# Where the next region's bias tiles stand among the column and row tiles of a sixteen-head mixing kernel

## The reference, cut to what matters

```python
h = relu(nd[..., None] * W1[0] + b1)          # nd: log distance, 0 above the diagonal
x = x + (einsum('qkm,mh->qkh', h, W2) + b2).transpose(2, 0, 1)
ret  = einsum('BGMTS,GMN->BGNTS', x, w + eye)
hq   = einsum('BGMTS,BTGIM->BGITS', x, qw1)   # a matrix for each row t
ret += einsum('BGITS,BTGIM->BGMTS', hq, qw2)
hk   = einsum('BGMTS,BSGIM->BGITS', x, kw1)   # a matrix for each column s
ret += einsum('BGITS,BSGIM->BGMTS', hk, kw2)
ret += x * qdd (by row) + x * kdd (by column)
```

## Time and profile before

| | before |
|---|---|
| median of three runs | 930.36 us (927.4 to 930.49) |
| profiled execution | 932.34 us |
| its span | 930.5 us |
| mean granted TensorE clock | 0.929 |
| TensorE matmul busy | 747.1 us (80%) |
| VectorE / ScalarE / GpSimd busy | 453.0 / 386.3 / 432.1 us |
| DMA moved | 149.63 MB, mean 161 GB/s |

### The profile page before, as it was taken

The page is one execution under the profiler, slowest core; times in us unless marked ns, Lnnn a source line. Parts: engine busy times, 40 slices in busy tenths (PEclk is TensorE's granted clock), DMA queues, the critical chain, the costliest instruction groups (busy, mean ns, idle before and its releaser), DMA issues.

```text
span 930.5 us, 39085 instructions
## 1 busy us (share of the span) xinstructions
PE 747.1 (80%) x18210; PEld 552.8 (59%) x18210; DVE 453.0 (49%) x483; ACT 386.3 (42%) x412; POOL 432.1 (46%) x267
## 2 busy tenths in 40 slices
PE   0667863898779877998899978988789886997974
PEld 0254642676557655766667655666557665766974
DVE  7496522376335543554336623554336542563343
ACT  3959413554445344543343334333434244431200
POOL 3546421254224422455568745675548654681020
PEclk9889977999989999998999999999889998999998
DMA  6786676839972999199844998389744998098068
GB/s 132 181 174 143 153 154 149 180 67 246 252 162 59 220 228 201 48 190 240 197 92 99 225 175 206 58 191 249 169 84 91 214 236 185 19 188 212 6 156 198
DMA packets 301054, 149.63 MB, mean 161 GB/s; under 512 B 30044, under 2 KB 296668, under 8 KB 300892
## 3 DMA queue, kind: packets, MB, share of 16 engines
q1 hardware_dynamic: 187552, 92.05, 45.3%
q10 hardware_dynamic: 113340, 55.08, 26.4%
HBM read 77.61 MB, written 69.47 MB: 158 GB/s over the span
## 4 chain that ended last, share of the span: by engine, by line
PE 70%; issue 12%; SPq 5%; DVE 4%; DMA 3%; ACT 2%; ACTq 2%; POOL 0%; DVEq 0%
PE main L755 27%; PE main L744 25%; PE bias L769 18%; SPq L326 4%; DMA homes<-in_x 2%; ACT homes L513 1%; ACTq L269 1%; DVE homes L299 1%; SPq L334 1%; DVE homes L601 1%; DMA out_mixed<-homes 1%; ACT hidden L502 1%; SPq L269 1%; DVE homes L604 0%; DVE w_blocks L626 0%
## 5 line engine op out<-in xcount | busy, mean ns | idle before, releaser
L463 POOL TENSOR_TENSOR hidden<-log_table,row_scale 128x1024 f32<-128x1024 f32 x192 | 364.4, 1912 | 366.9 <-PE bias L769 359.1
L755 PE MATMUL main<-homes,mats_b 32*32 32x120 f32 (+1 forms) x9216 | 286.6, 273 | 107.6 <-issue 80.1
L755 PEld LDWEIGHTS main<-homes,mats_b 32*32 32x32 f32 x9216 | 260.3, 133 | 173.0 <-issue 137.2
L502 ACT ACTIVATE hidden<-hidden,b_col 128x1024 f32<-128x1024 f32 x192 | 219.2, 1148 | 306.4 <-issue 154.6
L744 PEld LDWEIGHTS main<-homes,mats_a 32*32 32x32 f32 x8192 | 240.8, 129 | 87.1 <-issue 67.1
L744 PE MATMUL main<-homes,mats_a 32*32 32x128 f32 x8192 | 263.5, 276 | 28.6 <-issue 28.4
L669 DVE SCALAR_TENSOR_TENSOR homes<-bias,b_col,homes 64x512 f32<-64x512 f32 (+1 forms) x256 | 185.8, 747 | 119.5 <-PE bias L769 75.1
L769 PE MATMUL bias<-hidden,w_blocks 128*64 128x512 f32 x768 | 208.2, 646 | 19.1 <-ACT hidden L502 9.4
L651 DVE TENSOR_TENSOR homes<-main,homes 128x1024 f32<-128x1024 f32 x128 | 156.7, 1225 | 111.7 <-PE main L744 111.5
L641 DVE COPY homes<-main 128x960 f32<-128x960 f32 x64 | 74.1, 1158 | 231.8 <-PE main L755 231.7
L529 ACT ACTIVATE homes<-main 128x960 f32<-128x960 f32 (+1 forms) x80 | 71.0, 890 | 124.1 <-PE main L755 109.3
(11 more groups left out here) (37 smaller groups left out, 32.2 us busy)
## 6 DMA issues: line engine op xcount, KB each, us to landing
homes<-in_x SPq DMA_DIRECT2D x200, 192.0 KB, 6.7
out_mixed<-homes ACTq DMA_DIRECT2D x192, 192.0 KB
homes<-in_x SPq DMA_DIRECT2D x72, 256.0 KB, 7.2
out_mixed<-homes ACTq DMA_DIRECT2D x72, 128.0 KB, 4.5
homes<-in_x SPq DMA_DIRECT2D x136, 64.0 KB
mats_in<-a_mats SPq DMA_DIRECT2D x128, 64.0 KB
out_mixed<-homes ACTq DMA_DIRECT2D x28, 256.0 KB, 7.5
out_mixed<-homes SPq DMA_DIRECT2D x28, 256.0 KB, 6.7
```

The source lines that it names most:

```text
L463: nc.gpsimd.tensor_tensor(hidden_tile(u, g).rearrange("p (j s) -> p j s", j=ROWS), bass.AP(logs.tensor, logs.offset, [list(logs.ap[0]), [1 ...
L502: nc.scalar.activation(hidden_tile(u, g), hidden_tile(u, g), ACT.Relu, bias=b1_col[:, 0:1])\
L755: mm = pe.matmul(main[of_group(g), i % 2, j * W:j * W + REGION_TILES[k] * ROWS], b_weights(g, C * ROWS + j), y_column(k, g, C * ROWS + j), ...
```

## The change

`bias_step` gets other numbers for k of 1 and more; for k = 0 it stays. Before, the fifteen bias tiles stood after steps 1, 3, 5, ..., 29: eight behind column tiles, seven behind row tiles. Now tiles 0 to 9 stand after steps 1, 2, 4, 5, 7, 8, 10, 11, 13 and 14, two for every three column tiles, and tiles 10 to 14 after steps 17, 19, 21, 23 and 25. Steps 26 to 30 have none.

```diff
@@ -177,7 +177,10 @@
         def bias_step(k, T):
 
-            return 1 + T * (COL_TILES + REGION_TILES[k] - 3) // (REGION_TILES[k + 1] - 1)
+            if k == 0:
+                return 1 + T * (COL_TILES + REGION_TILES[k] - 3) // (REGION_TILES[k + 1] - 1)
+
+            return 1 + 3 * T // 2 if T < 10 else COL_TILES + 2 * (T - 10) + 1
```

## The result

| | before | changed |
|---|---|---|
| median of four runs | 930.24 us (927.40 to 930.49) | 957.52 us (947.98 to 982.57) |
| ratio of the fast runs | | 1.033, 95% interval 1.026 to 1.040 |
| profiled execution, its span | 932.34, 930.5 us | 954.62, 952.8 us |
| mean granted TensorE clock | 0.929 | 0.933 |

The changed kernel is 3% slower. The forecast was 956 us. The ratio leaves out the run of 982.57 us, a slow one; the two medians alone stand at 1.029. Timed once more, beside some of the experiments, the ratio was 1.040 (1.028 to 1.052). The experiments ran on three chips, where the times of a kernel spread by 2% and more, and are told in ratios to the kernel before on the same chip for that reason.

What follows compares the result with a forecast made beforehand. TensorE's order of work and its stops, read as instruction fetches, were taken to bound the kernel. Terms 12.4 + 0 + 10 + 3.5 = 26 us on 932.3 gave 958, median 956 us; range 922 to 978.

Steps and rivals of the forecast that it cites:

- a, the wait for hidden tiles: Column steps, regions 4 to 7: TensorE waits 1.55 us in close bias-tile pairs; eight of twenty counted, 12.4 us.
- the pairs there are covered: Column steps up to 9, regions 4 to 7: three of five close pairs hide within 6.7 us instruction blocks, uncounted.
- The bound of 31 us: Column steps, regions 4 to 7: all twenty waits of 1.55 us are paid if the cover fails.
- b, the two moved bias tiles: Seven regions, two bias tiles each from row to column steps: sum 0, bounds 21 us more or less.
- c, tile 14 and its x: Row steps, regions 1 to 7: bias tile after step 25 meets late x; 16 us summed, 10 taken.
- none in region 5: Row steps of region 5: VectorE does not wait for x before the bias addition after step 25.
- d, tile 1 and its x: Column steps, regions 1 and 5: TensorE stands one column tile earlier when late x lands, 3.5 us in all.
- The reading of the stops as code that arrives late: Column steps: TensorE's stops, 128 matmul records apart, are waits for the next 16 KB instruction packet among x loads.
- faster: Column steps: stops swallow the moved bias tiles and all waits there; 918 to 922 us, chance 0.14.
- Everything is paid: Whole kernel: stops aren't fetches, or come on top; 50 us more, 981 us, chance 0.12.
- The clock, which I feared for: Column steps: granted clock 0.88 against 1.00 in rows; twenty new stops could bring more slow work; no separate size.

## Why the prediction was right

Right was the time (957.5 us against 956; 954.6 against 958 for the profiled execution), the sign and the kind of three of its four terms. How close the number came is in part luck: the terms were off by several microseconds each, in both directions, and the ratio was 1.040, or 37 us, when the kernel was timed once more.

**a, the wait for hidden tiles: right in kind, wrong in how it is covered.** 5.1 to 5.2 us from bias tile to bias tile were worked out, 5.25 measured; 1.55 us of wait, 1.51 measured. The step that failed is "the pairs there are covered". The sum had nothing for the twelve pairs up to step 8 and 12.4 us for the eight behind them; 11.9 and 9.4 us were measured, 21.3 in all. What was covered is the account: the stops for code in those steps fell from 40.4 to 33.7 us (36.0 to 40.4 in three executions with the old places there, 27.9 to 33.7 in four with the new ones). Net 14.5 us, near the 12.4 counted, but put together otherwise. The bound of 31 us was nearly reached where little covers (28.6 us with short loads).

**b, the two moved bias tiles: near zero, as the sum had it.** The columns of k = 4 to 7 grew by 25.4 us; less 14.5 for a, 10.9 are left for eight bias tiles (15.0 us of work, 7.5 counted). The granted clock of these four stretches had been 0.88, 0.97, 0.86 and 0.94 and was 0.95, 0.95, 0.90 and 0.97, so slow work may have given back the difference. The rows shortened by 4.1 us with the late x in them, and with tile 14 back at step 29 they took 172.2 us, 8.7 less than before (7.5 counted).

**c, tile 14 and its x: right in kind and in the waits, not shown in the time.** By the same sum region for region, 3.3, 1.4, 0, 7 to 8, 0, 2.6 and 1.6 us stood in the prediction; 3.47, 0.42, 0, 7.80, 2.01, 1.94 and 2.03 were measured, 17.7 in all against 16. The sign "none in region 5" failed: VectorE waited 5.1 us there, TensorE 2.01. I took 6 us of the 16 to lie over stops for code, and more did. The row steps of k = 4 to 7 can be added up. 181.0 us less 15.0 for the bias tiles, plus 13.8 for the waits, with stops down from 8.2 to 5.9, make 177.5, and 176.9 were measured. With tile 14 back at step 29 there are no waits, the stops are 14.2, the sum is 172.0, and 172.2 were measured. So 13.8 us of waits cost 4.7 in these steps, where the prediction had counted ten sixteenths of them. (The second execution is from another chip.)

**d, tile 1 and its x: half.** Region 1's column steps grew by 2.6 us, one column tile and a little: ahead of the second late piece of x TensorE did one column tile less. The wait of region 5 in the earlier trace rows is chance: none of the four other profiled executions with the old places in region 5's columns has it, nor has the changed kernel's, while one with the new places has 10.4 us there. One row is not enough to count on.

**The reading of the stops as code that arrives late** carried the argument about cover. Two things are shown. One is the tie to the x loads: with an eighth of the bytes the stops in those columns were 9.1 us, not 40.4. The other goes beyond. Count TensorE's matmul records from the start of the program, and the stops fall behind the same counts in all thirteen profiled executions (give or take one record), whatever the order of the tiles: in the columns of region 4 behind 7839, 7967, 8094, 8222, 8349, 8477 or 8604 records, 127 or 128 apart. A stop stands behind 8349 records in eleven of the thirteen, and behind 12415, in region 6, in all of them. All 201 stops in these columns stand at such points. Moving the tiles changed what work stood there and which of these points became stops, not which points there are. So the stops belong to the place in TensorE's row of instructions and to no tile. That the thing waited for is code rests on this and on the instruction queue's packets; no run takes code away, so that last step is argued. The Trainium skill (Runtime: NRT & Kernel Launch, section on instruction fetch mechanics) has crossing a block mostly hidden. By the runs that is so with short x loads (9 us of stops in four regions' column steps) and not with full ones (40 us).

Of the rivals, "faster" fell because close pairs wait wherever they stand, and because the cover is some 16 us where 43 are added. "Everything is paid" (981 us) describes the columns of the kernel with short x loads, not this one. The clock, which I feared for, did not fall with the new waits: 0.933 against 0.929.

## What to carry to other kernels

Before moving work into idle time, work out the shortest distance that its own buffer ring allows between two pieces (release, refill, transform, use): here 5.2 us, and the even spread had 5.3. Bringing every second piece nearer cost a wait, and most of that was paid. Where idle time comes from late transfers, a new wait in it can be partly free even though it shows in full in the profile: look at what the other stops lose as well as at the wait, and take a wait away before you count it (17.7 us of waits for a late x went, and 12 us of other stops came). And whatever is moved earlier meets its inputs earlier: check the issue time of each in the queue that carries it.

## What the runs showed of the hardware

- Stops of TensorE that the profile names issue depend on other traffic: the same column steps had 40.4 us of them with full x loads and 9.1 us with an eighth of the bytes. In thirteen profiled executions with different orders of tiles they fell behind the same counts of matmul records, 127 or 128 apart in the column steps of k = 4 to 7.
- The two groups' matmuls of a bias tile appear side by side: records in pairs that start within 0.05 us, and the releases of both buffers 0.04 to 0.06 us apart (medians), the first 1.95 us behind the tile's start, in either order of the code.
- Waits of 1.5 us on TensorE, one every 10.5 us, left the granted clock of the column steps at 0.95 in region 4 (0.88 before, with its longer stops). With short x loads it was 1.00 in regions 5 to 7, with fifteen such waits and five other stops of 0.6 to 2.8 us, and 0.94 in region 4: there the clock was at its lower level for 6.8 us, from inside a stop of 3.38 us on, and at the higher one through the five waits.
